# Two units' q and k in one product of 512 columns

## The reference

```python
# layer 0: 12 heads of 32, masked attention inside each graph
q = split_heads(x @ Wq + bq); k = split_heads(x @ Wk + bk); v = split_heads(x @ Wv + bv)
scores = einsum('bhqd,bhkd->bhqk', q, k) / sqrt(32) + beta * adj
scores = where(adj > 0, scores, -9e15)
h = layernorm(x + merge_heads(softmax(scores) @ v))
# layer 1: two steps l = 0, 1 of
a = softmax(z @ z.T / sqrt(384)) * adj; attn = a / (a.sum(-1) + 1e-10)
ctx = (attn * upper) @ (z @ Wl.T + bl) + diag(attn) * (z @ Ws.T + bs) + (attn * lower) @ (z @ Wr.T + br)
z = relu(norm(ctx) * g + b)
out = layernorm(h + z)
```

## Time and profile before

| | |
|---|---|
| median of 3 runs | 1282.96 us (1282.18 to 1283.35) |
| the profiled execution | 1282.98 us, span of its instructions 1281.2 us |
| busy, share of the span | PE 99%, PEld (weight loads) 91%, DVE 77%, ACT 49%, POOL 29% |
| mean granted TensorE clock | 0.996 |
| mean DMA rate | 52 GB/s |
| instructions | 34717, of them 13844 matmuls |

### The profile page before, as it was taken

The page is one execution under the profiler, slowest core; times in us unless marked ns, Lnnn a source line. Parts: engine busy times, 40 slices in busy tenths (PEclk is TensorE's granted clock), DMA queues, the critical chain, the costliest instruction groups (busy, mean ns, idle before and its releaser), DMA issues.

```text
span 1281.2 us, 34717 instructions
## 1 busy us (share of the span) xinstructions
PE 1263.4 (99%) x13844; PEld 1166.7 (91%) x13844; DVE 990.4 (77%) x2691; ACT 632.6 (49%) x1338; POOL 370.6 (29%) x401
## 2 busy tenths in 40 slices
PE   9999999999999999999999999999999999999986
PEld 8999999999999999999999999999999999999975
DVE  6777778777878777787778787777877777877877
ACT  6544554544554445545445545455454455454543
POOL 3322323232323222323223232223232232323211
PEclk9999999999999999999999999999999999999989
DMA  8211110111110111110111101111101111011000
GB/s 275 85 39 57 58 57 25 35 57 57 57 57 4 55 57 57 57 28 31 57 58 58 57 15 44 57 57 57 43 16 57 57 58 58 20 39 45 26 14 26
DMA packets 53072, 66.34 MB, mean 52 GB/s; under 512 B 17840, under 2 KB 39856, under 8 KB 52784
## 3 DMA queue, kind: packets, MB, share of 16 engines
q1 hardware_dynamic: 52768, 63.93, 16.5%
q10 hardware_dynamic: 144, 0.20, 0.0%
HBM read 38.54 MB, written 12.58 MB: 40 GB/s over the span
## 4 chain that ended last, share of the span: by engine, by line
PE 97%; DVE 1%; issue 1%; ACT 1%; POOL 0%; POOLq 0%; DVEq 0%; ACTq 0%
PE bank L420 25%; PE bank L422 23%; PE bank L421 23%; PE bank L623 7%; PE bank L569 4%; PE bank L532 4%; PE bank L517 3%; PE bank L498 3%; PE bank L545 2%; PE bank L555 2%; PE bank L603 1%; PE bank L631 0%; DVE probs L1222 0%; POOL probs L1727 0%; PE bank L745 0%
## 5 line engine op out<-in xcount | busy, mean ns | idle before, releaser
L420 PE MATMUL bank<-w_hi,hT_hi 128*128 128x384 f32 x1158 | 405.4, 350 | 0.2 <-ACT hT_hi L1048 0.2
L422 PE MATMUL bank<-w_hi,hT_lo 128*128 128x384 f32 x1158 | 390.3, 337 | 0.0
L421 PE MATMUL bank<-w_lo,hT_hi 128*128 128x384 f32 x1158 | 390.1, 337 | 0.0
L420 PEld LDWEIGHTS bank<-w_hi,hT_hi 128*128 128x128 f32 x1158 | 218.3, 189 | 6.6 <-issue 2.0
L421 PEld LDWEIGHTS bank<-w_lo,hT_hi 128*128 128x128 f32 x1158 | 218.9, 189 | 0.0
L422 PEld LDWEIGHTS bank<-w_hi,hT_lo 128*128 128x128 f32 x1158 | 218.3, 189 | 0.0
L1293 DVE TENSOR_TENSOR hlr<-bank,rows 128x384 f32<-128x384 f32 x256 | 142.3, 557 | 70.9 <-PE bank L422 68.0
L1740 POOL TENSOR_TENSOR ln_rstd<-ln_var,minus_half 128x2 f32<-128x2 f32 x125 | 96.2, 769 | 322.1 <-DVE ln_var L1386 113.8
L1727 POOL TENSOR_TENSOR probs<-probs,row_max 128x768 f32<-128x768 f32 x64 | 94.6, 1478 | 265.7 <-DVE row_max L1228 265.7
L1310 DVE TENSOR_TENSOR late<-bank,rows 128x384 f32<-128x384 f32 x128 | 71.3, 558 | 118.0 <-PE bank L422 117.9
L420 PE MATMUL bank<-xT_hi,w_hi 128*128 128x256 f32 x558 | 158.7, 284 | 0.0
(11 more groups left out here) (131 smaller groups left out, 2370.9 us busy)
## 6 DMA issues: line engine op xcount, KB each, us to landing
v_halves<-v_stage SPq DMA_DIRECT2D x128, 99.0 KB, 2.3
x_in<-in_x SPq DMA_DIRECT2D x32, 384.0 KB, 4.0
xT_in<-in_xT SPq DMA_DIRECT2D x31, 384.0 KB, 3.4
out<-late SPq DMA_DIRECT2D x31, 384.0 KB, 2.4
late<-in_w SPq DMA_DIRECT2D x7, 576.0 KB, 6.5
adj_in<-in_adj SPq DMA_DIRECT2D x32, 96.0 KB, 3.8
adjT_in<-in_adjT SPq DMA_DIRECT2D x64, 48.0 KB, 3.2
rows<-in_vectors SPq DMA_DIRECT2D x1, 1536.0 KB, 8.7
```

The costliest lines, as they stand in the source:

```text
L420: nc.tensor.matmul(o, l_hi, r_hi, start=first and n == 0, stop=False)
L421: nc.tensor.matmul(o, l_hi, r_lo, start=False, stop=False)
L422: done = nc.tensor.matmul(o, l_lo, r_hi, start=False, stop=final and n == last)
```

## The change

q and k are no longer made for one unit in its own EARLY step. Units 1 to 30 form pairs (1, 2), (3, 4), ... (29, 30); for a pair, the weight block stays the stationary operand and the x of both units are the moving one, 512 columns in one matmul, one whole PSUM bank for a group. A pair has six groups; three (j = 0, 1, 2) are made in the step whose EARLY is the pair's first unit less one, three in the step whose EARLY is its first unit. Units 0 and 31 stay alone, with 256 columns; unit 31's groups are spread over two steps in the same way. Pair (1, 2) has all six in `second`, where v of unit 1 now comes before the groups and ScalarE's and GpSimd's orders are written anew. x is split two steps sooner (stage SPLIT = 4), into three slots of `xT_hi` and `xT_lo`, and loaded two steps sooner (LOAD = 5). q and k get separate tiles with slots for a pair and for the next (`q_first`, `k_first`, `q_second`, `k_second`), and ScalarE takes each group with two ACTIVATEs of 256 columns, one a unit. The scratch for DMAs that GpSimd would issue is set to 4096 bytes.

```diff
+SPLIT, LOAD = 4, 5
+X_SLOTS = 3
+GROUPS = 2 * KC
+def qk_set(unit):
+    return (unit + 1) // 2
+def set_units(p):
+    first = max(2 * p - 1, 0)
+    return [u for u in (first, first + 1) if u < UNITS and qk_set(u) == p]
+def x_slot(unit):
+    return (unit - 1) % X_SLOTS
+def step_groups(unit):
+    return [(qk_set(unit + 1), j) if unit % 2 == 0 else (qk_set(unit), KC + j) for j in range(KC)]
...
-        kT = sb("kT", [P, KC, TOK])
+        k_first = sb("k_first", [P, 1, 3, TOK])
+        k_second = sb("k_second", [P, 2, 2, TOK])
...
-        xT_hi = sb("xT_hi", [P, KC, TOK], F32R)
-        xT_lo = sb("xT_lo", [P, KC, TOK], F32R)
-        qT = sb("qT", [P, KC, TOK])
+        xT_hi = sb("xT_hi", [P, KC, X_SLOTS, TOK], F32R)
+        xT_lo = sb("xT_lo", [P, KC, X_SLOTS, TOK], F32R)
+        q_first = sb("q_first", [P, 2, 3, TOK])
+        q_second = sb("q_second", [P, 1, 2, TOK])
...
+        def group_bank(p, j):
+            return SECOND_QK_BANKS[j % 2] if p == 1 else QK_BANKS[j % KC]
+        def x_of_set(p, kc):
+            at = sorted(x_slot(u) for u in set_units(p))
+            every = at[-1] - at[0] if len(at) > 1 else 1
+            return tuple(tile[:, kc, at[0]:at[-1] + 1:every, :] for tile in (xT_hi, xT_lo))
...
+            def project_qk(st, p, j):
+                units, m = set_units(p), j // 2
+                pe.wait_ge(xhi_ready, units[-1] + 1)
+                pe.wait_ge(xlo_ready, units[-1] + 1)
+                if p == 1:
+                    if j == 0:
+                        need(pe, s_masked, st.count(MID, 4, 4))
+                    if j >= 2:
+                        pe.wait_ge(qk_ready, qk_taken(p, j - 2))
+                elif j % KC == KC - 1:
+                    pe.wait_ge(qk_ready, qk_taken(p, j - 1))
+                o = group_bank(p, j)[:, 0:len(units) * TOK].rearrange("p (u n) -> p u n", u=len(units))
+                done = product(o, [(weight((W_Q, W_K)[j % 2], kc, m * P, (m + 1) * P), x_of_set(p, kc)) for kc in range(KC)])
+                done.then_inc(qk_psum, 1)
...
             def second(st):
                 scores(st, MID)
                 project_v(st, MID)
-                project_qk(st, 0)
+                project_v(st, EARLY)
+                project_qk(st, 1, 0)
+                project_qk(st, 1, 1)
                 transpose_probs(st)
-                project_qk(st, 1)
+                project_qk(st, 1, 2)
                 attend(st)
-                project_qk(st, 2)
-                project_v(st, EARLY)
+                project_qk(st, 1, 3)
+                project_qk(st, 1, 4)
+                project_qk(st, 1, 5)
                 transpose_h(st)
                 scores(st, EARLY)
...
+                    groups = step_groups(st.unit(EARLY))
                     project_v(st, EARLY)
-                    project_qk(st, 0)
-                    project_qk(st, 1)
+                    project_qk(st, *groups[0])
+                    project_qk(st, *groups[1])
                 if late:
                     transpose_z(st)
                 if mid:
                     transpose_probs(st)
                 if early:
-                    project_qk(st, 2)
+                    project_qk(st, *groups[2])
...
+            def split_x(unit):
+                act.wait_ge(xT_loaded[unit % 2], 16 * (unit // 2 + 1))
+                held = unit - X_SLOTS
+                if held >= 1:
+                    act.wait_ge(qk_psum, qk_made(qk_set(held), GROUPS - 1))
+                    act.wait_ge(v_psum, 2 * (held + 1))
+                    act.wait_ge(xlo_ready, held + 1)
+                nc.scalar.activation(xT_hi[:, :, x_slot(unit), :], xT_in[:, unit % 2], ACT.Copy).then_inc(xhi_ready, 1)
...
+            def take_qk(st, p, j):
+                m = j // 2
+                act.wait_ge(qk_psum, qk_made(p, j))
                 need(act, s_psum, st.count(MID, 1, 1))
+                for unit in set_units(p):
+                    bias, scale = (bk_col, 1.0) if j % 2 else (bq_col, SCALE_ATT)
+                    nc.scalar.activation(group_out(unit, j), group_half(unit, group_bank(p, j)), ACT.Identity,
+                                         bias=bias[:, m:m + 1], scale=scale).then_inc(qk_ready, 1)
...
             def second(st):
-                split_x(st)
+                split_x(1)
+                split_x(2)
                 split_weight(3)
                 split_weight(4)
                 exp_scores(st, 0)
                 exp_scores(st, 1)
+                take_qk(st, 1, 0)
+                take_qk(st, 1, 1)
                 take_pT(st)
-                take_qk(st, 0)
+                take_qk(st, 1, 2)
                 split_weight(5)
-                take_qk(st, 1)
-                take_qk(st, 2)
+                take_qk(st, 1, 3)
+                take_qk(st, 1, 4)
                 normalize_h(st)
+                take_qk(st, 1, 5)
                 take_hT(st)
                 split_hT(st)
+                split_x(3)
...
+            def second(st):
+                split_x(1)
+                split_x(2)
+                shift_scores(st, 0)
+                shift_scores(st, 1)
+                split_adj(st)
+                add_x(st)
+                inverse_root(st, MID, 1, 1, ln0_eps, ln0_var, ln0_rstd, ln0_rs)
+                split_x(3)
...
-    nc = bacc.Bacc("TRN2", target_bir_lowering=False, num_devices=1)
+    nc = bacc.Bacc("TRN2", target_bir_lowering=False, num_devices=1, dynamic_dma_scratch_size=4096)
```

More of the change, by code:

```diff
@@ L313, in _, with load_xT @@
         def _(sp):
-            def load_xT(st, ahead):
-                need(sp, xlo_ready, st.count(ahead - 2, 1, 1))
-                slot = st.slot(ahead)
-                sp.dma_start(xT_in[:, slot], xT[st.unit(ahead)]).then_inc(xT_loaded[slot], 16)
+            def load_xT(unit):
+                if unit >= 2:
+                    sp.wait_ge(xlo_ready, unit - 1)
+                sp.dma_start(xT_in[:, unit % 2], xT[unit]).then_inc(xT_loaded[unit % 2], 16)
             def load_x(st, ahead):
@@ L394, in step @@
                     return
-                if st.has(EARLY + 1):
-                    load_xT(st, EARLY + 1)
+                if st.has(LOAD):
+                    load_xT(st.unit(LOAD))
                 if st.has(MID + 1):
@@ L475, in project_qk @@
                             pe.wait_ge(xlo_ready if last else x0_lo_set, 1 if last else kc + 1)
[L476 removed]
+                        done = product(o, [(weight(wn, kc, m * P, (m + 1) * P), (x0_hi[:, kc, :], x0_lo[:, kc, :]))],
                                        first=kc == 0, final=kc == KC - 1)
[L478 removed]
+                    if m == KC - 1 and n == 0:
                         done.then_inc(q0_psum, 1)
                 done.then_inc(qk_psum, 1)
+            def project_qk(st, p, j):
[12 more added lines that the diff above has]
+                done.then_inc(qk_psum, 1)
             def scores(st, stage):
[L483 removed]
+                unit = st.unit(stage)
+                pe.wait_ge(qk_ready, qk_taken(qk_set(unit), GROUPS - 1))
                 if st.unit(stage) >= 2:
@@ L510, in transpose_probs @@
                     need(pe, v_staged, st.count(EARLY, 2, 2))
-                    need(pe, qk_ready, st.count(EARLY, 6, 2))
+                    pe.wait_ge(qk_ready, qk_taken(*step_groups(st.unit(EARLY))[0]))
                 for t in range(T):
@@ L537, in transpose_h @@
             def transpose_h(st):
-                if st.has(EARLY):
-                    need(pe, qk_ready, st.count(EARLY, 6, 6))
+                if st.unit(MID) == 0:
+                    need(pe, v_staged, st.count(MID, 2, 2))
+                elif st.has(EARLY):
+                    pe.wait_ge(qk_ready, qk_taken(*step_groups(st.unit(EARLY))[-1]))
                 need(pe, pT_ready, st.count(MID, 3, 3))
@@ L634, in begin @@
             def begin(st):
-                for m in range(3):
-                    project_qk(st, m)
+                for m in range(KC):
+                    project_first_qk(m)
             def second(st):
@@ L867, in take_qk @@
-            def take_qk(st, m):
-                if st.unit(EARLY) == 0 and m == 0:
+            def split_x(unit):
[6 more added lines that the diff above has]
+                nc.scalar.activation(xT_hi[:, :, x_slot(unit), :], xT_in[:, unit % 2], ACT.Copy).then_inc(xhi_ready, 1)
@@ L1096, in step @@
                     return
+                if early:
+                    groups = step_groups(st.unit(EARLY))
                 if late and st.unit(LATE) == 0:
@@ L1104, in step @@
                     scale_turned(st, 0)
-                elif early:
-                    split_x(st)
+                elif st.has(SPLIT):
+                    split_x(st.unit(SPLIT))
                 if late and st.unit(LATE) != 0:
@@ L1778, in step @@
                     return
-                if early and not st.unit(EARLY) == 0:
-                    split_x(st)
+                if st.unit(EARLY) == 0:
+                    return
+                if st.unit(MID) == 0:
```

(4 more changed lines are left out.)

116 lines of the change are left out of this document (56 added, 60 removed).

## The result

The changed kernel takes 1287.25 us (median of six runs, 1286.61 to 1288.2) against 1282.72 us (1281.83 to 1283.35) of the kernel before in the same comparison: ratio 1.0039, 95% interval 1.0028 to 1.0051. It is 4.5 us, 0.4%, slower. The forecast was 1281.2 us, range 1277.3 to 1286.0; the time lies outside, on the slow side.

The account below looks back on a forecast made before the run. TensorE, busy 99% of the span, was taken to bound the kernel. Steady steps -4.5, second step +5.2 and last two EARLY steps -2.5 summed to -1.8 us against 1282.98, so 1281.2 us, range 1277.3 to 1286.

Parts of the forecast that it names:

- the missing price: Distance between 512-column products, absent from the trace: taken as 226.7 ns from the 384-column row, 223 to 231 likely.
- the prediction's own turn of 0.81 us per ns: Whole kernel: the total turns by 0.81 us for each ns of 512-column distance, over 810 products.
- A: 28 steady steps: groups 0 and 1 save 0.16 us a step, the third group nothing; -4.5 us.
- B: Second step, making all six groups of units 1 and 2: more product work less stalls, +5.2 us, range 4.8 to 6.2.
- the prediction's own signs of being wrong: New profile: TensorE idle in a steady step, distance outside 223 to 231 ns, or last two steps under 37 us.
- All TensorE: Steady steps: 38.87 us each, 28 times, with TensorE never idle.
- the free edits: Steady steps: ScalarE copies, moved x splits and loads, two-piece reads, strided slots and smaller DMA scratch put at nothing.
- the covers: Second step: slack for unit 2's x, GpSimd's adjacency split and the third x split; a failure costs 0.2 to 1 us, once.
- C: Last two steps with EARLY (30 and 31): 3.2 us less work each, but TensorE waits for other engines; -2.5 us.
- Rival 2: 512-column products: width buys nothing, 236 ns (two pieces, whole bank), 1288.8 us; decides from 232 ns; chance 0.12 with neighbours.
- The line through 113.8 and 173.6: 512-column products: straight-line extrapolation from the 256- and 384-column distances, giving 233 ns.
- distances 228 to 231: Slower rival: such 512-column distances, or more stalls in the second step, give 1282 to 1285 us; chance 0.15.

Follow-up runs that it names:

- streams alone: Matmul streams on TensorE with nothing of the layers computed, at several widths and tile places; output zeros, time means nothing; first set gave 226.7 ns for 512 columns.
- the stream above: Changed kernel with 54 more products ahead of the first group in ten steps, here 384 columns of the pair: 176.7 ns apart; some 12 us longer per stream.
- The extra products: Changed kernel with the first q and k group made twice in the steps with EARLY = 30 and 31: the two steps took 37.32 + 37.85 us.
- the 18 streams: TensorE streams without the layers, x and weights moved against each other to 18 places in SBUF: 512 columns 226.7 to 236.7 ns, 256 columns 116.7 to 123.3.

## Why the prediction was wrong, and where it was right

- **The step that failed is the missing price.** "I take 226.7, next to the nearest row", and the argument that 384 columns pay an excess of 13.6 ns which is close to saturated. In streams alone at place 0 that was right to the digit (226.7), but the kernel does not stand there, so the agreement is in part luck. The price is not one number: it depends on where the two operands lie against each other modulo 256 bytes, and the change kept x at 192, where 512 columns cost 233.3 and 256 columns 117.8. Nearest in width and type was not enough: in the row of 384 columns the weights move and h, which lies as x does, is stationary, so moving less stationary is 64 there, where 512 columns cost 228.9. With x moving at 192, as the change has it, 384 columns cost 176.7 (the stream above), and that excess of 16.7 ns carried to 512 columns gives 230, an estimate from the nearer row. By the prediction's own turn of 0.81 us per ns, 6.7 ns are +5.4 us, of the 6.0 by which the median missed; as measured by parts, A missed by 4.6 and B by 1.4. A distance outside 223 to 231 was among the prediction's own signs of being wrong.
- **Settling was put at nothing**, since the price was taken for every product. With x at the cheap place the prediction's A still came out at -2.6 us (late by 6.63 us at unit 1's attention, 4.02 at unit 28's), not -4.5, and the kernel at 1284.42, 3.2 us above the forecast.
- **A** (-4.5): measured +0.1. A steady step was to be 38.87 and is 39.04; 27 products times 6.7 ns are 0.18. "All TensorE" and the free edits held: TensorE does not wait in these steps, and with narrow products in the new schedule the step is 39.03, so copies, splits and the smaller scratch cost nothing there; the stream in two pieces cost what the one in one piece did.
- **B** (+5.2, range 4.8 to 6.2): measured +6.6 at unit 1's attention. The gram came 0.36 late against it, just 54 x 6.7 ns. The wait for the last copy of k was there (0.27). The rest, 1.0 us, is the third step: the stall of 0.99 us, in no term of the sum, less the wait for VectorE that shrank from 0.55 to 0.09 us, and 0.31 more in front of the transposes of the probabilities (0.65 against 0.34); 0.16 is left over. The third x split, named among the covers, did make exp of the gram late (42.40 instead of 41.16 without that split), but by another way than feared: ScalarE had its part done at 40.39 and then waited 2.01 us for u_bias, which GpSimd's part held up. TensorE lost nothing visible by it.
- **C** (-2.5): measured -2.4. Two reliefs of about 1.2 us, with the waits where they were placed: pT, then VectorE's low half of z. The extra products confirmed it: 2.1 us of work for 0.19 us.
- **Rival 2** had the right outcome, 0.12 of the chance, 1288.8. Its mechanism, two pieces and a whole bank, is wrong: a stream with both stands at 226.7 ns. It put the border at 232 ns, and the 233.3 measured are over it.
- **The range** reached to 1286.0 and left most of rival 2 out. The line through 113.8 and 173.6 gave 233, and "distances 228 to 231" had 0.15: of the ways to extrapolate three pointed above 226.7, one at it, one below. That spread was in the text and deserved more weight than 0.12.

No version beat the kernel before. The best pair kernel is the one with x moved, 1284.42 us. The streams show 116.7 ns for 256 columns at 16 and 32 bytes instead of 117.8; on the kernel before this would be 36 x 1.1 ns = 0.04 us a step, if the third group's 113.3 stayed, and was not run.

## What to carry to other kernels

When a change rests on the price of a matmul shape that the trace does not have, measure that shape at the addresses that the kernel will give it; a few bytes between the tiles of the two operands can be worth as much as the change. Moving work from the end of a pipeline to its head costs full price at the head, and at the end it gives back only what TensorE was really the last to finish. Compare a shape change and a schedule change separately: with narrow products in the new schedule the first run would have shown that all of the loss was the schedule's.

## What the runs showed of the hardware that I had not expected

- The distance of float32r matmuls with a weight load each depends on the place (moving less stationary operand) modulo 256 bytes in SBUF: 512 columns 226.7, 228.9, 232.0 to 232.5, 233.3 ns at 0, 64, 128, 192; 256 columns 120.0, 117.8, 118.9 to 120.0, 117.8; 384 columns, with the weights as the moving operand, 173.3, 173.3, 175.7 to 176.2, 174.7. One element (4 bytes) off 0 is the worst of the 18 streams: 236.7 and 123.3.
- It takes about ten products to settle behind a stream of another shape, and the same stream may settle at another value behind another start: in the kernel before, 256 columns stand 117.8 apart behind v and 113.3 behind transposes. In the second step of the kernel with narrow products 54 of them behind attention stay at 113.3 to the end (30.55 to 36.80 us), and 36 behind v at 117.8. With x moved to 0 both are 120.0. Why there are two values is open.
- A matmul of 16 columns with its own weights costs 108 ns in a stream.
- TensorE stood still for 0.9 to 4.3 us for no semaphore, near a fetch of a block of its instructions; 48 instructions more ahead moved the stall and made it four times as long, and the granted clock fell to 0.50 behind it, from 46 to 52 us.
- GpSimd's split of x (1.9 us) held up a VectorE instruction on two values for 1.74 us instead of 0.17. The Trainium skill, SBUF — State Buffer, section on the two separate sides, says that these two engines share a pair of ports, and that a GpSimd instruction, or a VectorE one of certain kinds, holds it for the whole instruction while the other waits. The rows agree in time: u_bias ends at 42.36 us, the split at 42.34. Which mode u_bias ran in, no view shows.
